# Two Flamingo layers in one kernel: the expert stage's first product takes both parts of its input in one matmul

## The reference, cut to what matters

```python
t = x.reshape(-1, D)                                  # 8192 x 512, layer-normed
probs = jax.nn.softmax(t @ Wr, axis=-1); idx = jnp.argmax(probs, -1)   # one expert per token
# up to cap = int(1.25 * N / E) = 1280 tokens of each expert are gathered, then for expert e:
h = jax.nn.relu(tokens_e @ W1[e])                     # 512 -> 2048
eout = h @ W2[e]                                      # 2048 -> 512
out = where(kept, eout, t) * where(kept, pmax, 1)
x = x + tanh(g_ffn[1]) * out
```

## Time and profile before

| | |
|---|---|
| median of 3 runs | 2019.31 us (2018.92 to 2020.88) |
| the profiled execution's own time | 2018.42 us |
| its span, first to last instruction | 2016.7 us |
| mean granted TensorE clock | 0.98 |
| TensorE matmul busy | 1920.3 us, 95% |
| VectorE busy | 953.5 us, 47% |
| ScalarE busy | 742.3 us, 37% |
| GpSimd busy | 759.5 us, 38% |
| DMA | 208.79 MB, mean 104 GB/s |

### The profile page before, as it was taken

One profiled execution on the slowest core, in us unless ns is written; L12 is line 12 of the kernel. 1 busy time (PEld: TensorE's weight loads), 2 busy tenths in 40 slices (PEclk: granted clock), 3 DMA queues, 4 the chain that ended last, 5 costly groups with the idle time before them and its releaser, 6 DMA issues.

```text
span 2016.7 us, 34799 instructions
## 1 busy us (share of the span) xinstructions
PE 1920.3 (95%) x10956; PEld 1630.0 (81%) x10957; DVE 953.5 (47%) x2245; ACT 742.3 (37%) x1711; POOL 759.5 (38%) x803
## 2 busy tenths in 40 slices
PE   5899999999999389999999999999999999999997
PEld 3677777777776279898899989998898998899986
DVE  6879999999985733324121332124133214121331
ACT  3446666666565322414111231124123114111331
POOL 5656675675652322415211241124224115211340
PEclk9999999999999699999999999999999999999999
DMA  7323443533534551505201250115124115101220
GB/s 241 110 87 126 158 148 126 174 132 126 183 122 166 169 174 55 175 29 171 76 27 35 65 169 26 36 42 173 52 72 157 31 32 183 52 31 31 92 75 11
DMA packets 152911, 208.79 MB, mean 104 GB/s; under 512 B 13472, under 2 KB 79264, under 8 KB 152839
## 3 DMA queue, kind: packets, MB, share of 16 engines
q1 hardware_dynamic: 111767, 114.15, 17.9%
q0 software_dynamic: 15728, 43.38, 7.1%
q10 hardware_dynamic: 25344, 50.33, 7.0%
HBM read 140.98 MB, written 68.37 MB: 104 GB/s over the span
## 4 chain that ended last, share of the span: by engine, by line
PE 82%; DVE 7%; issue 5%; ACT 1%; DVEq 1%; DMA 1%; POOL 1%; SPq 0%; ACTq 0%; POOLq 0%
PE bank L782 25%; PE bank L790 24%; PE bank L1527 7%; PE bank L1445 7%; PE bank L750 6%; PE bank L730 6%; PE bank L1499 2%; DVE x2T_lo L1855 1%; PE bank L708 1%; PE bank L739 1%; PE bank L1453 1%; DVE xdT_lo L1855 1%; DMA stage<-in_L_ffn_W_dram 1%; DVE a_m L1874 0%; DVE up_lo L1846 0%
## 5 line engine op out<-in xcount | busy, mean ns | idle before, releaser
L890 DVE SCALAR_TENSOR_TENSOR hT_lo<-bank,hT_hi 128x256 fp32r<-128x256 f32 x352 | 149.4, 424 | 678.6 <-ACT hT_hi L658 677.6
L658 ACT ACTIVATE hT_hi<-bank 128x256 fp32r<-128x256 f32 x352 | 134.9, 383 | 754.0 <-PE bank L782 744.5
L782 PE MATMUL bank<-inT_hi,w_hi 128*128 128x256 f32 x1408 | 399.7, 284 | 0.6 <-DVEq L938 0.6
L782 PE MATMUL bank<-inT_hi,w_lo 128*128 128x256 f32 x1408 | 400.0, 284 | 0.0
L782 PE MATMUL bank<-inT_lo,w_hi 128*128 128x256 f32 x1408 | 396.7, 282 | 0.0
L790 PE MATMUL bank<-w_hi,hT_hi 128*128 128x512 f32 x704 | 280.8, 399 | 0.0
L782 PEld LDWEIGHTS bank<-inT_lo,w_hi 128*128 128x128 f32 x1408 | 266.3, 189 | 14.5
L790 PE MATMUL bank<-w_lo,hT_hi 128*128 128x512 f32 x704 | 277.9, 395 | 0.0
L790 PE MATMUL bank<-w_hi,hT_lo 128*128 128x512 f32 x704 | 277.6, 394 | 0.0
L782 PEld LDWEIGHTS bank<-inT_hi,w_hi 128*128 128x128 f32 x1408 | 266.0, 189 | 13.9 <-DVEq L938 1.0
L782 PEld LDWEIGHTS bank<-inT_hi,w_lo 128*128 128x128 f32 x1408 | 265.2, 188 | 0.0
(11 more groups left out here) (314 smaller groups left out, 3805.3 us busy)
## 6 DMA issues: line engine op xcount, KB each, us to landing
stage<-in_L_ffn_W_dram SPq DMA_DIRECT2D x256, 256.0 KB, 3.0
X<-in_x_dram SPq DMA_DIRECT2D x16, 1024.0 KB, 5.7
t_d<-tt ACTq DMA_DIRECT2D x16, 1024.0 KB
x_d<-x ACTq DMA_DIRECT2D x16, 1024.0 KB, 6.7
out_dram<-y ACTq DMA_DIRECT2D x16, 1024.0 KB, 8.4
xs<-in_x_dram SPq DMA_DIRECT2D x16, 768.0 KB
cw_a<-in_L_xattn_conv_w_dram SPq DMA_DIRECT2D x2, 1024.0 KB, 10.0
cw_b<-in_L_xattn_conv_w_dram SPq DMA_DIRECT2D x2, 1024.0 KB, 15.0
```

Of the source, the lines that this page charges most:

```text
L658: act.activation(hT_hi[:, f % 4, :], hb[f % 4][:, 0:CN], ACT.Relu).then_inc(e_hh, 1)
L782: last = pe.matmul(hb[f % 4][:, 0:CN], l[:, k, fs], r[:, k, :], start=(n == 0), stop=(n == 3 * KB - 1))
L890: dve.scalar_tensor_tensor(out=hT_lo[:, f % 4, :], in0=hb[f % 4][:, 0:CN], scalar=0.0, in1=hT_hi[:, f % 4, :].bitcast(F32), op0=ALU.max, o ...
```

## The change

1. The high and low part of a chunk's input lie beside each other (`inT`), and `first_product` multiplies W1's high part with both in one matmul of 512 columns: high x high goes to the left half of the bank, high x low to the right half, and low x high (256 columns) to the right half too. ScalarE then copies the right half out (`part`), VectorE adds it to the left half, and the Relu follows; in an expert's last chunk, the next expert's high parts are made between the copy and the Relu.
2. TensorE reads the next expert's four numbers inside the last chunk, at f = 3, 6, 9 and 12. The loop over experts 1 to 6 is written out on TensorE.
3. Where the experts begin, TensorE, ScalarE and GpSimd read their first numbers earlier. The last group's x3 store is issued one pipeline step earlier, before its t store; its y store later, behind the first unit's input on ScalarE. VectorE makes the low parts of blocks 4 to 7 ahead of the last planning steps, not behind.
4. `e_out` counts halves of a chunk's result; the very last `put` waits for one half at a time.

```diff
@@ expert stage's memory
-            inT_hi = eb("inT_hi", [P, KB, CN], F32R)
-            inT_lo = eb("inT_lo", [P, KB, CN], F32R)
+            inT = eb("inT", [P, KB, 2, CN], F32R)
+            inT_hi, inT_lo = inT[:, :, 0, :], inT[:, :, 1, :]
@@ GpSimd, experts_on_gpsimd
                 pool.wait_ge(c_v, UNITS_PLANNED)
+                at = load(pool, unit_col[:, ds(0, 1)], NC - 1)
                 pool.wait_ge(e_slots, 16)
                 pool.wait_ge(s_t, 16 * NG)
-                unit_inputs(0)
+                unit_inputs(0, at)
...
-                pool.wait_ge(e_out, all_c + 1)
-                settled(pool)
                 for i in range(CH):
+                    pool.wait_ge(e_out, all_c * CH + (i + 1))
+                    settled(pool)
                     put(ob[:, i, :], idx_x[:, i:i + 1], e_sc)
@@ ScalarE, chunk
                         act.wait_ge(e_m1, c * FB + f + 1)
+                        act.activation(part[:, f % 2, :], hb[f % 4][:, CN:2 * CN], ACT.Copy).then_inc(e_part, 1)
+                        if following is not None and f > BEHIND:
+                            split_high(following, f - BEHIND - 1, c)
+                        act.wait_ge(e_sum, c * FB + f + 1)
                         if f >= 4:
                             act.wait_ge(e_m2, c * FB + f - 3)
                         act.activation(hT_hi[:, f % 4, :], hb[f % 4][:, 0:CN], ACT.Relu).then_inc(e_hh, 1)
-                        if following is not None and f > BEHIND:
-                            split_high(following, f - BEHIND - 1, c)
@@ ScalarE, experts
+                    act.wait_ge(c_v, UNITS_PLANNED)
+                    begin, end = expert_units(act, 0)
                     unit_inputs(0)
+                    act.wait_ge(g_y, T * NG)
+                    act.dma_start(of[ds((NG - 1) * G, G), :].rearrange("(j p) e -> p j e", p=P),
+                                  y[:, :, :]).then_inc(s_y, 16)
                     for f in range(RING + 4, FB):
...
-                    begin, end = expert_units(act, 0)
@@ TensorE, first_product
+                    both = hb[f % 4][:, :].rearrange("p (w c) -> p w c", w=2)
                     for k in range(KB):
-                        for l, r in ((w1_hi, inT_hi), (w1_hi, inT_lo), (w1_lo, inT_hi)):
-                            last = pe.matmul(hb[f % 4][:, 0:CN], l[:, k, fs], r[:, k, :], start=(n == 0), stop=(n == 3 * KB - 1))
-                            n += 1
+                        if k == KB - 1:
+                            pe.matmul(hb[f % 4][:, CN:2 * CN], w1_lo[:, k, fs], inT[:, k, 0, :], start=False, stop=False)
+                        last = pe.matmul(both, w1_hi[:, k, fs], inT[:, k, :, :], start=(k == 0), stop=(k == KB - 1))
+                        if k < KB - 1:
+                            pe.matmul(hb[f % 4][:, CN:2 * CN], w1_lo[:, k, fs], inT[:, k, 0, :], start=False, stop=False)
@@ TensorE, chunk
+                        if following is not None:
+                            if f == 3:
+                                begin_next = load(pe, unit_first[:, ds(following, 1)], MAXU)
+                            ... (f == 6, 9 and 12: the other three)
@@ TensorE, the experts
+                pe.wait_ge(c_v, UNITS_PLANNED)
+                begin, end = expert_units(pe, 0)
                 turn_unit(0)
                 pe.wait_ge(c_v, PLANNED)
-                begin, end = expert_units(pe, 0)
...
-                with pe.Fori(1, E - 1) as e:
-                    begin, end = expert_units(pe, e)
-                    first_c, last_c = expert_chunks(pe, e)
+                for e in range(1, E - 1):
                     with pe.Fori(begin, end) as u:
                         unit(e, u, first_c)
                     with pe.Fori(first_c, last_c) as c:
                         chunk(e, c, end)
-                    chunk(e, last_c, end)
+                    begin, end, first_c, last_c = chunk(e, last_c, end, e + 1)
@@ VectorE, chunk
                     for f in range(FB):
+                        dve.wait_ge(e_part, c * FB + f + 1)
+                        dve.tensor_tensor(hb[f % 4][:, 0:CN], hb[f % 4][:, 0:CN], part[:, f % 2, :],
+                                          ALU.add).then_inc(e_sum, 1)
                         dve.wait_ge(e_hh, c * FB + f + 1)
@@ VectorE, experts
-                    for f in range(RING // 2, RING):
-                        first_low(1, f)
-                        first_low(2, f)
                     unit_inputs(0)
@@ ScalarE, token stage, step of group e (its stores) and of group d
-                    if d is not None:
-                        wait(act, v_x3, T * d + 1)
-                    act.dma_start(x3_d[ds(er, G), :]...).then_inc(s_x3, 16)
+                    if not final(e):
+                        (the same)
-                if e is not None:
+                if e is not None and not final(e):
                     wait(act, g_y, T * (e + 1))
                     act.dma_start(of[ds(er, G), :]..., y[:, :, :]).then_inc(s_y, 16)
+                if final(d):
+                    act.wait_ge(v_x3, T * NG)
+                    act.dma_start(x3_d[ds(d * G, G), :]...).then_inc(s_x3, 16)
@@ VectorE, plan
-                    for f in range(RING // 2):
+                    for f in range(RING):
                         low(1, f)
                         if f >= 2:
                             low(2, f)
```

More of the change, by code:

```diff
@@ L397, in flamingo_two_layers @@
             ob = eb("ob", [P, CH, D], F32)
+            with nc.sbuf_tensor("part", [P, 2, CN], F32) as part:
+                pass
             huT_hi = eb("huT_hi", [P, 2, FQ, P], F32R)
@@ L530, in chunk @@
                     chunk_inputs(c + 1)
[L531 removed]
+                    pool.wait_ge(e_out, (c + 1) * CH)
                     settled(pool)
@@ L792, in second_product, with chunk @@
                     last.then_inc(e_m2, 1)
-                def chunk(e, c, end):
+                def chunk(e, c, end, following=None):
+                    begin_next = end_next = first_next = last_next = None
                     for f in range(FB + BEHIND):
+                        if following is not None:
+                            if f == 3:
+                                begin_next = load(pe, unit_first[:, ds(following, 1)], MAXU)
+                            if f == 6:
+                                end_next = load(pe, unit_first[:, ds(following + 1, 1)], MAXU, 1)
+                            if f == 9:
+                                first_next = load(pe, chunk_first[:, ds(following, 1)], MAXC)
+                            if f == 12:
+                                last_next = load(pe, chunk_last[:, ds(following, 1)], MAXC)
                         if f < FB:
@@ L823, in experts_on_tensor @@
                     chunk(0, c, end)
-                chunk(0, last_c, end)
-                with pe.Fori(1, E - 1) as e:
-                    begin, end = expert_units(pe, e)
-                    first_c, last_c = expert_chunks(pe, e)
+                begin, end, first_c, last_c = chunk(0, last_c, end, 1)
+                for e in range(1, E - 1):
                     with pe.Fori(begin, end) as u:
@@ L831, in experts_on_tensor @@
                         chunk(e, c, end)
-                    chunk(e, last_c, end)
-                begin, end = expert_units(pe, E - 1)
-                first_c, all_c = expert_chunks(pe, E - 1)
+                    begin, end, first_c, last_c = chunk(e, last_c, end, e + 1)
                 with pe.Fori(begin, end) as u:
                     unit(E - 1, u, first_c)
-                with pe.Fori(first_c, all_c) as c:
+                with pe.Fori(first_c, last_c) as c:
                     chunk(E - 1, c, end)
@@ L899, in chunk @@
                     for i in range(CH):
-                        done = dve.scalar_tensor_tensor(out=ob[:, i, :], in0=acc[i][:, :], scalar=gp[:, i:i + 1],
-                                                        in1=xg[:, i, :], op0=ALU.mult, op1=ALU.add)
-                    done.then_inc(e_out, 1)
+                        dve.scalar_tensor_tensor(out=ob[:, i, :], in0=acc[i][:, :], scalar=gp[:, i:i + 1],
+                                                 in1=xg[:, i, :], op0=ALU.mult, op1=ALU.add).then_inc(e_out, 1)
                     if following is not None:
@@ L1314, in body @@
                     act.dma_start(t_d[ds(er, G), :].rearrange("(j p) e -> p j e", p=P), tt[:, :, :]).then_inc(s_t, 16)
-                    if d is not None:
-                        wait(act, v_x3, T * d + 1)
-                    act.dma_start(x3_d[ds(er, G), :].rearrange("(j p) e -> p j e", p=P),
-                                  x3[:, ds(xe, T), :]).then_inc(s_x3, 16)
+                    if not final(e):
+                        if d is not None:
+                            wait(act, v_x3, T * d + 1)
+                        act.dma_start(x3_d[ds(er, G), :].rearrange("(j p) e -> p j e", p=P),
+                                      x3[:, ds(xe, T), :]).then_inc(s_x3, 16)
```

15 lines of the change are left out of this document (9 added, 6 removed).

## The result

| | before | after |
|---|---|---|
| median | 2020.10 us (4 runs, 2018.92 to 2021.02) | 1994.34 us (4 runs: 1989.78, 1993.43, 1995.25 and 2798.51) |
| the profiled execution | 2018.42, span 2016.7 | 1995.25, span 1993.2 |
| mean granted TensorE clock | 0.98 | 0.98 |

The ratio is 0.9865 (95% 0.9846 to 0.9885); the execution of 2798.51 us ran at a granted clock of 0.65 and is left out of the ratio (the other three have the median 1993.43). The same kernel once more gave 1992.47 us against 2020.47, a ratio of 0.9866 (0.9849 to 0.9882). The forecast was 1997.2.

What follows compares the result with a forecast made beforehand. It took TensorE's distance between matmul starts in the expert stage as the bound. 13.4 + 5.0 + 3.0 + 0.7 = 22.1 us off the profiled 2018.42 gave 1996.3, or 1997.2 for the median; range 1990 to 2007.

Steps and rivals of the forecast that it cites:

- Both parts in one product: First product in the chunks: 9.5 ns saved in each of 1408 steps, 13.4 us (bounds 5.6 to 16.9).
- I take 230.5: Price in ns of a 512-column matmul interleaved with 256s, between 228 in a row and 232 inside a chunk.
- 8 to 12 ns are a fixed cost of each start: TensorE's matmuls: every start costs some 8 to 12 ns that does not grow with columns, from 120 and 228 to 232.
- The chain at chunk starts: Copy, add, Relu and low part take 1.74 us at a chunk's start; 0.86 us left, no stall at 22 starts.
- The w_lo that falls wrong: VectorE's w_lo ahead of an add in an expert's last chunk: at most 0.6 us per expert, taken as 0.
- Reads between blocks: TensorE's reads of four numbers and loop jump between experts: 5.0 us gained, lower bound 4.0.
- First expert: Opening: earlier x3 store brings slots 2.8 us earlier and hu 2.4 to 3.3 earlier; 3.0 us gained.
- by some 2 us, under the same wait, so nothing of their own: TensorE's two reads ahead of `turn_unit(0)` bring its own two products forward some 2 us, counted as no gain.
- VectorE's and GpSimd's work is only in another order: Opening at the first expert: reordering work on these two engines was given no cost or gain.
- End: The final `put` of ob waits for one half, not both: 0.7 us gained.
- Instruction fetch: Unrolled code for five more experts: fetches costed at nothing; as a rival, 30 fetches give 2027 us, chance 0.03.
- 2 (the y store): ScalarE's wait for the y store decides the first expert: nothing won or 2 us lost there, 2001 us; chance 0.12.

Runs made afterwards that it cites:

- unroll_only: Kernel before with TensorE's loop over experts written out, the four reads still between experts: 2015.1 us, against 2020.2 beside it.
- after_again: The changed kernel, unaltered, timed and profiled once more: 1992.47 us, ratio 0.9866 to the kernel before.
- wide_first: Changed kernel with each block's four wide matmuls ahead of the four narrow ones, not in turns: 1996.63 us.
- pairs_apart: Changed kernel with two of a block's four merged matmuls (k = 1 and 2) split again into two of 256 columns: 1999.92 us.
- opening_only: Kernel before with only item 3 of the change, the work ahead of the first unit: 2018.11 us, ratio 0.9988.
- chain_longer: Changed kernel with three more ScalarE copies of 128x256, output unused, ahead of each chunk's first block: 1994.51 us.
- x3_back: Changed kernel with the last group's x3 store again behind its t store: 1993.38 us, one run.
- merge_only: Kernel before with only item 1, the merged product; TensorE's experts stay in a loop with the reads between them: 2007.19 us, ratio 0.9934.
- reads_only: Kernel before with only item 2, reads inside the last chunk and the loop over experts written out: 2015.94 us, ratio 0.9971.
- low_parts_back: Changed kernel with VectorE's low parts of blocks 4 to 7 again behind the last planning steps: 1995.79 us, one run.

## Why the prediction was right

It said 1997.2 us and 22.1 us gained; the profiles' segments have 28.3. Term by term:

- **Both parts in one product**, forecast 13.4 us, measured 24.1 − 5.1 = 19.0. The gain comes where it was forecast, in the chunk's blocks, and the term was too small. Mean distances of starts over all blocks inside chunks add up to 1438 ns for the old first product and 1396 for the new: 43 before rounding, where the forecast had 4 x 9.5 = 38. That is 15.1 us for 352 blocks. The second product, which the change doesn't touch, went from 1402 to 1388: 14 ns, 4.8 us; together 19.9, against 19.0 by the segments. "I take 230.5" held, with 230.3 measured. What failed are the prices kept beside it: the 256-column matmuls went from 120 to 118.6, and the second product was left out of the sum. That 8 to 12 ns are a fixed cost of each start, the reason given for the term, is not borne out (the table of four kernels above): a block is 14 ns shorter for each merged matmul, and why is open.
- **The chain at chunk starts**, forecast without a stall: none, with about 0.8 us to spare (forecast 0.86), and 0.43 us for the add as taken. The w_lo that falls wrong, forecast at 0 with up to 0.6 us an expert, cost one block 0.3 us in one of the two profiles.
- **Reads between blocks**, forecast 5.0, measured 5.1 (6.74 − 1.62), all passages at 0.23. But the 5.0 was the cost in the old kernel. With the merged product it would have been 12.38 − 1.62 = 10.8: the forecast lacks the step that item 1 makes the passages longer. It held because item 2 takes away whatever stands there. And it named the reads and the jump together; unroll_only shows that writing the loop out was enough.
- **First expert**, forecast 3.0, measured 3.5, by a largely wrong way, so the size is luck. The slots came 3.3 us earlier (forecast 2.8) and hu 3.7 (3.0). But hu held TensorE for 1.0 us only; a longer wait stood ahead of it. TensorE's waits in before, 700 to 745 us:

```profile
PE bank L730 <- DVE w_lo L913: 3.6, 1, 3.6
PE bank L739 <- ACT hu L632: 1.0, 1, 1.0
```

  The first is put down to VectorE, but the sequencer's records show TensorE's own four reads of numbers there, 705.45 to 709.59: the product starts at 710.16, 2.15 us behind the end of its input's low part (708.01). After, two reads stand ahead of the turned tokens, and the product starts 0.14 us behind that low part, 1.95 us earlier from T0. With 1.01 for hu and an estimated 0.36 for a shorter stretch at the low clock that is 3.3 of the 3.5. The step that failed is that the two reads bring the products forward "by some 2 us, under the same wait, so nothing of their own": the 2 us were right and counted in full, and hu's earlier start, priced at 3.0, could give 1.0. "VectorE's and GpSimd's work is only in another order" failed too: GpSimd's copy lost 4.4 us beside VectorE's row, so the unit's tokens came no earlier.
- **End**, forecast 0.7, measured 0.65.
- **Instruction fetch**, forecast at nothing: 63 packets against 41, and no wait on TensorE beside those shown.

Of the rivals, 2 (the y store) had a point: ScalarE is done with the weights at 30.0 after T0 and starts hu at 33.25, 0.3 us after y has landed (32.95). But it costs nothing, since TensorE doesn't wait for hu in that profile. The signs that the forecast named came out (blocks 2.79 apart, line 730's entry gone, no wait for hT_lo, first chunk 3 us earlier). Its absolute times for the slots (691.8) and hu (715.5) did not, 695.8 and 719.3, since T0 was 4.5 later; from T0 they are 0.5 and 0.7 us better than forecast. Read by the letter, a sign of being wrong came out too: ScalarE waited for the y store past 718, to 719.0. Counted from T0 that is 714.5 on the old profile's clock.

## What to carry to other kernels

Where matmuls run back to back, read the distance of starts at two widths. Twice the narrow minus the wide is a first estimate of what a merge saves (8 to 12 ns here, 14 measured); measure the block around it too, since its neighbours change with the order. Take a hardware loop and its reads off the issuing queue before you make the chain ahead of them longer, because both draw on the same queued work. When a wait ahead of a stage is what you shorten, read the granted clock behind it as well. And compare profiles by segments from a common event, over several profiles, since start and opening can drift by more than a term of the sum.

## What the runs showed of the hardware

- At a granted clock of 1.0, a block of matmuls took 2783 ns with 8 matmuls in its first product in turns of width, 2796 with the wide ones of the same 8 first, 2800 with 10 and 2840 with 12 (after_again, wide_first, pairs_apart, before). pairs_apart against after_again makes 8.5 ns for each start more, pairs_apart against wide_first 2, where the forecast's other figure, from the Trainium skill ("TensorE: Matmul & The Clock Gate", "Wait — 56ns, not 53.3ns?"), is about 2.5.
- Narrow and wide matmuls in turns start closer (118.6 and 230.3 ns behind each) than in rows of their own (119.4 and 231.7).
- A GpSimd copy of 128x1 took 4.85, 4.93, 5.06, 4.85, 3.68 and 1.68 us (after, after_again, opening_only, chain_longer, pairs_apart, x3_back), each ending 0.05 us behind the end of an unbroken row of 128x512 VectorE subtractions. It took 0.27 to 0.47 us beside such a row in five others (before, merge_only, reads_only, unroll_only, wide_first), ending 0.05 us behind the subtraction that ran when it came, and 0.18 to 0.35 where the row had ended or paused.
- TensorE's outer loop, with four reads of numbers in it, cost 0.85 us at a passage (1.08 against 0.23) in the old product, though matmuls were queued ahead of it.
- TensorE's granted clock fell from 1.0 to 0.5 during a wait of 3.9 us for hu, between 717 and 718 us, and was back at 1.0 at 725 (low_parts_back).
